# A fused attention and local-attention block: mask, maximum, token shift and value copies each moved to another engine

## What is computed

```python
h = shift_token(x)                      # second half of the channels comes from the token before
q, k, v = split(h @ wqkv)               # 8 heads x 64
q, k = l2norm(q) * qs, l2norm(k) * ksc  # then a rotary turn
sim  = einsum('bhwid,bhwjd->bhwij', bq * 8, bk)   # window of 64 queries x 128 keys
mask = (i < j) | (i > j + WINDOW) | (j == -1)
attn = softmax(where(mask, -max, sim))
x = x + (attn @ bv) @ wo
h = layernorm(shift_token(x))           # the second token shift
x = x + (a * gelu(g)) @ w2 + b2         # a, g = split(h @ w1 + b1)
```

## Time and profile before

| | before |
|---|---|
| median of 3 runs | 2481.74 us (2478.46 to 2484.01) |
| the profiled execution's own time | 2479.8 us |
| its span | 2478.0 us, mean granted clock 0.979 |
| PE busy | 2243.9 us, 91% |
| PEld busy | 1567.1 us, 63% |
| DVE busy | 1675.2 us, 68% |
| ACT busy | 1702.9 us, 69% |
| POOL busy | 1771.1 us, 71% |
| local-attention tiles | 128, the first masked at 222.7 us, the last at 2438.0 us |

### The profile page before, as it was taken

One profiled execution on the slowest core, in us unless ns is written; L12 is line 12 of the kernel. 1 busy time (PEld: TensorE's weight loads), 2 busy tenths in 40 slices (PEclk: granted clock), 3 DMA queues, 4 the chain that ended last, 5 costly groups with the idle time before them and its releaser, 6 DMA issues.

```text
span 2478.0 us, 59154 instructions
## 1 busy us (share of the span) xinstructions
PE 2243.9 (91%) x22208; PEld 1567.1 (63%) x22208; DVE 1675.2 (68%) x3612; ACT 1702.9 (69%) x2766; POOL 1771.1 (71%) x1615
## 2 busy tenths in 40 slices
PE   4888999999999999999999999999999999988887
PEld 1454666676666666666676666666666666665665
DVE  3666766777676776777667676677667766556653
ACT  1455677677777777767777776776777777776663
POOL 2117777786877868777777867777777877788883
PEclk9899999999999999999999999999999999999998
DMA  4221001110110110111011001011111100000000
GB/s 136 62 66 53 29 26 29 44 34 20 42 32 27 36 38 27 26 47 33 22 34 42 27 29 38 22 41 36 33 27 31 45 23 19 8 12 12 2 3 12
DMA packets 74966, 81.99 MB, mean 33 GB/s; under 512 B 7545, under 2 KB 64294, under 8 KB 74674
## 3 DMA queue, kind: packets, MB, share of 16 engines
q1 hardware_dynamic: 74674, 78.04, 11.0%
HBM read 56.26 MB, written 20.97 MB: 31 GB/s over the span
## 4 chain that ended last, share of the span: by engine, by line
PE 50%; ACT 18%; DVE 12%; issue 10%; POOL 8%; DMA 1%; SPq 0%; DVEq 0%; ACTq 0%; POOLq 0%
PE ps L540 8%; PE ps L633 6%; PE ps L825 4%; PE ps L588 4%; PE ps L573 3%; PE ps L700 3%; ACT PT L1188 3%; PE ps L739 3%; PE ps L553 3%; PE ps L722 2%; PE ps L816 2%; DVE ss L1027 2%; DVE nmax L976 2%; POOL inv L1407 2%; PE ps L687 2%
## 5 line engine op out<-in xcount | busy, mean ns | idle before, releaser
L976 DVE TENSOR_REDUCE nmax<-ps 128x1 f32<-128x512 f32 (+3 forms) x1024 | 471.6, 485 | 383.2 <-PE ps L575 380.4
L1188 ACT ACTIVATE PT<-ps 128x512 f32<-128x512 f32 (+1 forms) x768 | 407.0, 533 | 327.7 <-PE ps L590 323.3
L1407 POOL TENSOR_TENSOR inv<-ss,nhalf 128x16 f32<-128x16 f32 x128 | 378.7, 2959 | 322.3 <-DVE QN L1010 322.3
L573 PE MATMUL ps<-KA,QA 72*128 72x512 bf16 (+3 forms) x1024 | 290.2, 310 | 38.4 <-DVE nmax L976 33.1
L1396 POOL TENSOR_TENSOR RS<-RAW,rot 128x512 f32<-128x512 f32 x256 | 324.9, 1290 | 0.0
L1402 POOL TENSOR_TENSOR RC<-RC,RS 128x1024 f32<-128x1024 f32 x128 | 304.0, 2375 | 18.9 <-POOL RS L1396 1.3
L1385 POOL TENSOR_TENSOR RC<-RAW,rot 128x1024 f32<-128x1024 f32 x128 | 307.9, 2405 | 0.0
L588 PE MATMUL ps<-QA,KA 75*128 75x512 bf16 (+3 forms) x1024 | 285.6, 305 | 19.5 <-ACT PT L1188 15.4
L687 PE MATMUL ps<-wqkv,ZT 128*128 128x512 f32 x512 | 242.8, 597 | 0.0
L1246 ACT COPY V_odd<-ps 128x512 f32<-128x512 f32 x128 | 74.9, 585 | 217.1 <-PE ps L700 216.5
L1017 DVE TENSOR_REDUCE nm<-ps 128x8 f32<-128x1024 f32 x128 | 156.2, 1220 | 96.1 <-PE ps L722 95.1
(11 more groups left out here) (130 smaller groups left out, 5674.6 us busy)
## 6 DMA issues: line engine op xcount, KB each, us to landing
QA<-parts SPq DMA_DIRECT2D x192, 96.0 KB
KA<-parts SPq DMA_DIRECT2D x192, 96.0 KB
parts<-qkp SPq DMA_DIRECT2D x32, 384.0 KB, 5.5
X_next<-in_x SPq DMA_DIRECT2D x17, 256.0 KB, 2.9
X<-in_x SPq DMA_DIRECT2D x16, 256.0 KB, 3.0
x_kept<-X SPq DMA_DIRECT2D x16, 256.0 KB, 3.0
XR<-x_kept SPq DMA_DIRECT2D x32, 128.0 KB, 3.7
out<-XR SPq DMA_DIRECT2D x32, 128.0 KB, 1.9
```

The lines of the kernel that those rows point to most:

```text
L573: pe.matmul(dst[:, c0:c0 + w], QA[e][0:QK_ROWS, h % UNIT, qt * P:(qt + 1) * P], KA[e][0:QK_ROWS, h % UNIT, 0:w], start=True, stop=False)
L976: ins = v.tensor_reduce(nmax[:, NT - 1 - r, h % H1:h % H1 + 1], for_max(i, x)[:, c0:c0 + w], AX.X, ALU.max, negate=True)
L1188: a.activation(PT1[:, h % UNIT, c0:c0 + w], for_exp(i, x)[:, 0:w], ACT.Exp, scale=SCALE1).then_inc(exped.sem, 1)
L1407: g.tensor_tensor(inv[:, :], ss[:, :], nhalf[:, :], ALU.pow).then_inc(inv_ready.sem, 1)
```

## The change

- `scores`: the two mask matmuls go. One matmul of a single column stands in their place, and each score matmul starts and stops its own accumulation.
- `maxima`: DVE adds `band` to the scores on their way from PSUM into `PX`, and then reduces `PX` in SBUF to `nm`.
- `exps`: eight exponentials, one for each head of 128 columns, each with its column of `nm` as bias.
- `shift_tokens` leaves PE for SP: two transfers within SBUF, of 127 rows and of 1 row. The DVE copy goes. `norms` and the statistics of the shifted half are split into calls of their own, and `tile_moments` comes after `gate_up` and `heads_over_sum`.
- `v_over`: one copy, to `V_odd`. SP moves its halves to the `V_even` buffers (`move_values`).
- `scores_max` and `scores_exp`: where a chunk holds two tiles, their two causal masks become one matmul of 256 columns.
- POOL: `tile_root` comes after `rotate_by_sin` and the sum.

```diff
+                def move_values(m):
+                    sp.wait_ge(*past(v_ready.sem, v_ready.at(i, m + 1)))
+                    for n, rows in enumerate((slice(0, WIN), slice(WIN, P))):
+                        sp.dma_start(V_even[(m + n) % 2][rows, :, :], V_odd[rows, :, :]).then_inc(v_moved.sem, 16)
+
+                def shift_tokens(m):
+                    l, z, tt = place(m)
+                    dst = XN[m // HT % 2][:, m % HT, D // 2:D]
+                    sp.wait_ge(*past(z_acc.sem, z_acc.at(i, m + 1)))
+                    sp.dma_start(dst[1:P, :], Z[z][0:P - 1, tt, D // 2:D]).then_inc(shifted.sem, 16)
+                    first = Z[z][P - 1:P, tt - 1, D // 2:D] if tt else ident[0:1, D // 2:D]
+                    sp.dma_start(dst[0:1, :], first).then_inc(shifted.sem, 16)
...
+                    if tile_in(i, s - 1):
+                        shift_tokens(s - 1)
                     if s % 2 == 0:
                         u = s // 2 + 10
                         if unit_in(i, u):
                             lay_maxima(u)
                         if unit_in(i, u + 2):
                             lay_out(u + 2)
+                    if tile_in(i, s + 1):
+                        move_values(s + 1)
...
-                                  KA[e][0:QK_ROWS, h % UNIT, 0:w], start=True, stop=False)
-                        last = pe.matmul(dst[:, c0 + w - P:c0 + w], identb[:, :], causal[:, :],
-                                         start=False, stop=True)
-                    last.then_inc(scored.sem, 1)
+                                  KA[e][0:QK_ROWS, h % UNIT, 0:w], start=r == CHUNKS[c][0], stop=False)
+                    n = len(CHUNKS[c])
+                    diagonal = dst[:, c0 + w - n * P:c0 + w].rearrange("p (t x) -> p t x", x=P)
+                    pe.matmul(diagonal, identb[:, :], causal[:, :].unsqueeze(1).to_broadcast([P, n, P]),
+                              start=False, stop=True).then_inc(scored.sem, 1)
...
-                    rows = band[:, 0 if tt else 1, :].unsqueeze(1).to_broadcast([P, PAIR2, P])
-                    for s in range(2):
-                        pe.matmul(ps[:, 2 + s, :], identb[:, :], rows, start=True, stop=False)
+                    pe.matmul(ps[:, 2, 0:1], identb[:, :], band[:, 0, 0:1], start=True, stop=True)
...
-                                               QT[half, j, b * WIN:(b + 1) * WIN], keys, start=False,
-                                               stop=j == PAIR2 - 1)
+                                               QT[half, j, b * WIN:(b + 1) * WIN], keys, start=True, stop=True)
...
-                def shift_tokens(m):
-                    l, z, tt = place(m)
-                    pe.wait_ge(*past(z_acc.sem, z_acc.at(i, m + 1)))
-                    dst = m_ps[:, D:D + D // 2]
-                    mm = pe.matmul(dst, shift[:, :], Z[z][:, tt, D // 2:D], start=True, stop=(tt == 0))
-                    if tt:
-                        mm = pe.matmul(dst, corner[:, :], Z[z][:, tt - 1, D // 2:D], start=False, stop=True)
-                    mm.then_inc(sh_mm.sem, 1)
...
                 def maxima(m):
-                    blocks = sc_ps.rearrange("p (h c) -> p h c", h=H2)
+                    l, z, tt = place(m)
+                    in_heads = "p (h c) -> p h c"
                     v.wait_ge(*past(s_mm.sem, s_mm.at(i, m + 1)))
-                    v.tensor_reduce(nm[:, :], blocks, AX.X, ALU.max, negate=True).then_inc(max_ready.sem, 1)
-                    v.wait_ge(*past(max_ready.sem, max_ready.at(i, m + 1)))
                     v.wait_ge(*past(p_tr.sem, p_tr.at(i, m)))
-                    v.tensor_tensor(PX.rearrange("p (h c) -> p h c", h=H2), blocks,
-                                    nm[:, :].unsqueeze(2).to_broadcast([P, H2, P]),
-                                    ALU.add).then_inc(sub_ready.sem, 1)
+                    v.tensor_tensor(PX.rearrange(in_heads, h=H2), sc_ps.rearrange(in_heads, h=H2),
+                                    band[:, 0 if tt else 1, :].unsqueeze(1).to_broadcast([P, H2, P]),
+                                    ALU.add).then_inc(banded.sem, 1)
+                    v.wait_ge(*past(banded.sem, banded.at(i, m + 1)))
+                    v.tensor_reduce(nm[:, :], PX.rearrange(in_heads, h=H2), AX.X, ALU.max,
+                                    negate=True).then_inc(max_ready.sem, 1)
...
+                def shifted_tokens(m):
+                    l, z, tt = place(m)
+                    v.wait_ge(*past(shifted.sem, shifted.at(i, 2 * (m + 1))))
+                    v.bn_stats(stats[z][:, tt, 6:12], XN[m // HT % 2][:, m % HT, half:D]).then_inc(tile_stats.sem, 1)
...
                     attention_step(s, 3)
+                    if tile_in(i, s + 3):
+                        norms(s + 3)
                     if tile_in(i, s - 1):
-                        tile_moments(s - 1)
-                    elif tile_in(i, s + 3):
-                        norms(s + 3)
+                        shifted_tokens(s - 1)
                     if b:
                         gate_up(p, 0)
                         gate_up(p, 1)
                     if s % 2 and unit_in(i, (s + 17) // 2):
                         heads_over_sum((s + 17) // 2)
+                    if tile_in(i, s - 1):
+                        tile_moments(s - 1)
...
                 def exps(m):
-                    a.wait_ge(*past(sub_ready.sem, sub_ready.at(i, m + 1)))
-                    a.activation(PX, PX, ACT.Exp).then_inc(exp_ready.sem, 1)
+                    a.wait_ge(*past(max_ready.sem, max_ready.at(i, m + 1)))
+                    for h in range(H2):
+                        block = PX[:, h * P:(h + 1) * P]
+                        ins = a.activation(block, block, ACT.Exp, bias=nm[:, h:h + 1])
+                    ins.then_inc(exp_ready.sem, 1)
...
-                    a.copy(V_odd[:, :, 0:E2], heads)
-                    a.copy(V_even[m % 2][0:WIN, :, 0:E2], heads[0:WIN, :, :])
-                    a.copy(V_even[(m + 1) % 2][WIN:P, :, 0:E2], heads[WIN:P, :, :]).then_inc(v_ready.sem, 1)
+                    a.wait_ge(*past(v_moved.sem, v_moved.at(i, 2 * m)))
+                    a.copy(V_odd[:, :, 0:E2], heads).then_inc(v_ready.sem, 1)
...
+                    if tile_in(i, s + 2):
+                        rotate_by_sin(s + 2)
                     if tile_in(i, s - 1):
                         tile_root(s - 1)
-                    if tile_in(i, s + 2):
-                        rotate_by_sin(s + 2)
```

More of the change, by code:

```diff
@@ L192, in build @@
         band = sb("band", [P, 2, P], BF16)
-        shift = sb("shift", [P, P])
-        corner = sb("corner", [P, P])
         cos1 = sb("cos1", [P, S])
@@ L360, in build @@
         v_ready = count("v_ready", ITEMS)
+        v_moved = Landed(nc, ctx, "v_moved", 2 * ITEMS)
         s_mm = count("s_mm", ITEMS)
         max_ready = count("max_ready", ITEMS)
-        sub_ready = count("sub_ready", ITEMS)
+        banded = count("banded", ITEMS)
         exp_ready = count("exp_ready", ITEMS)
@@ L373, in build @@
         z_acc = count("z_acc", ITEMS)
-        sh_mm = count("sh_mm", ITEMS)
-        sh_ready = count("sh_ready", ITEMS)
+        shifted = Landed(nc, ctx, "shifted", 2 * ITEMS)
         tile_stats = count("tile_stats", ITEMS)
@@ L391, in build @@
         y_out = landed("y_out", LANES)
-        N_FIRST, N_CONST = 4, 12 + L * 7
+        N_FIRST, N_CONST = 4, 10 + L * 7
         N_MADE = LANES + 9
@@ L416, in _ @@
                 (causal_t[:, :], t["causal_t"]), (band[:, :, :], t["band"]),
-                (shift[:, :], t["shift"]), (corner[:, :], t["corner"]),
                 (wqkv[:, :, :], t["wqkv"].rearrange("l d n -> d l n")),
@@ L588, in scores_exp @@
                         pe.matmul(dst[:, c0:c0 + w], KA[e][0:ROWS, h % UNIT, kt * P:(kt + 1) * P],
-                                  QA[e][0:ROWS, h % UNIT, kt * P:S], start=True, stop=False)
-                        last = pe.matmul(dst[:, c0:c0 + P], identb[:, :], causal_t[:, :],
-                                         start=False, stop=True)
-                    last.then_inc(scored_t.sem, 1)
+                                  QA[e][0:ROWS, h % UNIT, kt * P:S], start=kt == CHUNKS[c][0], stop=False)
+                    n = len(CHUNKS[c])
+                    diagonal = dst[:, 0:c0 + P].rearrange("p (t x) -> p t x", x=P)[:, ::NT - 1, :]
+                    pe.matmul(diagonal, identb[:, :], causal_t[:, :].unsqueeze(1).to_broadcast([P, n, P]),
+                              start=False, stop=True).then_inc(scored_t.sem, 1)
                 def turn_maxima(s, u):
@@ L734, in attend @@
                     pe.wait_ge(*past(pt_ready.sem, pt_ready.at(i, m + 1)))
-                    pe.wait_ge(*past(v_ready.sem, v_ready.at(i, m + 1)))
+                    pe.wait_ge(*past(v_moved.sem, v_moved.at(i, 2 * (m + 1))))
                     for h in range(H2):
@@ L759, in tokens_over @@
                     if tile_in(i, s - 1):
-                        pe.wait_ge(*past(sh_ready.sem, sh_ready.at(i, s)))
```

(23 more changed lines are left out.)

## The result

The changed kernel takes 2515.8 us (median of 4 runs, 2513.7 to 2518.6) against 2482.4 us for the kernel before on the same chip: ratio 1.0142, 95% interval 1.0118 to 1.0166. It is slower, and 2515.8 lies inside the range; but the growth is 33 us by the medians and 35 by the ratio, where the forecast of 2500 stood 18 above the median of before, and on the profiled executions it is 38.7 us (span 2516.7 against 2478.0) where the terms gave 20.

The account below looks back on a forecast made before the run. ACT's queue was taken to bind odd slots, mostly PE the even ones; +2.8 us a turn gave +18, the last pair +2, so +20 on 2479.8: forecast 2500, own range 2486 to 2530, full range 2405 to 2570.

Parts of the forecast that it names:

- The step on which the sign hung: Odd slots, `exps` to `last_chunk`: ACT's queue binds, so eight exponentials delay `last_chunk` by 1.4 us; faster below 1.15 of growth.
- 0.97: Growth of each odd slot: 1.4 us later on ACT, less 0.43 saved on PE's mask; eight make +7.8 a turn.
- the 2.6 counted for the copies: Start of `values`, where PE waits for ACT: two copies fewer on ACT a slot save 2.6 us a turn.
- some 100 were named: PE over the whole run: busy time was to fall by some 100 us, idle time to grow by more.
- The shift's transfer: SP's 127-row transfer, ahead of DVE's statistics: lands in 5.2 us on one DMA engine, just hidden within about 5.8.
- the rival of the late transfer: Shift's rows at 58 ns a packet land 3.1 us late, DVE stands: +32 us a turn, 2740; chance 0.09.
- the price of POOL's and DVE's new order in the even slots: Two even slots with 0.7 us of slack: `gate_up` behind L1030 takes the bank's gain, +0.2 us a turn.
- the full part lies above its forecast: First tile at 222 us to about 2136: 6.55 turns at +2.8 us, so +18 us.
- The clock: Rival: PE's new idle time lowers its clock, each 0.01 costing 3 us a turn; 2520 to 2560, chance 0.07.
- the 2.3 of the forecast: Slot 8 gains 2.3 us: 0.9 from POOL, 0.5 as the slot before ends later, 0.85 from PE.
- forecast 2.8: One turn of the loop, 16 slots: the terms of odd slots, even slots, slot 8 and copies sum to +2.8 us.
- The tail: Last pair, 8 pairs of slots: POOL's chain binds even slots (-0.6 each), ACT odd ones (+0.8): +2 us.

Follow-up runs that it names:

- e1: The changed kernel with the eight exponentials by head replaced by one over 1,024 columns, using the first head's negated maximum as bias: 2444.5 us, ratio 0.987.
- e2: The changed kernel with the old order back: moments ahead of `gate_up` on DVE, `tile_root` between the rotations on POOL: 2525.2 us, ratio 1.019.
- e3: The changed kernel with DVE's `next_sin` (rope sum) of slots 4 and 12 moved behind `add_mlp`: 2498.1 us, ratio 1.009.
- e5: The changed kernel with the token shift back on PE and its copy back on DVE: 2526.3 us, ratio 1.018.
- e8: The kernel before with only exponentials by head out of PSUM, maximum as bias, so DVE's second pass goes: 2519.5 us, ratio 1.016.
- e10: The changed kernel with the loop over pairs 1 to 5 written out, so no engine jumps back: 2491.6 us, ratio 1.003.
- e7: The changed kernel with mask on PE, one exponential, later rope sum, and POOL's `first_normalise` moved behind slot 8's maxima parts: 2442.6 us, ratio 0.985.
- e12: The changed kernel with mask on PE, later rope sum, no loop; exponentials by head from PSUM in even tiles, one in odd: 2385.8 us, ratio 0.961.

## Why the prediction was right in direction and too small

**Right.** The step on which the sign hung held: ACT's queue binds odd slots, and the growth was sized at 1.4 us and measured at 1.39; e1 takes it away and gives 67 us back. From the start of `exps` to the next `maxima` seven odd slots grew by 0.79 to 0.95 us (0.88 in the mean) against 0.97. Where odd slots begin, `exps` starts 3.2 us sooner, summed over a turn, against the 2.6 counted for the copies; that it is the copies isn't shown, as no run took them back alone. PE's busy time fell by 85 us, where some 100 were named. The shift's transfer was hidden in the full part. DVE waits for it, 3.65 us each time, only in the last four tiles. It was priced at 5.2 us (its own terms, 1.4 us and 127 packets of 29 ns, give 5.1) and lands sooner; in the drain, where it can be followed alone:

```profile
2491.17 0.63 SPq L490
2491.80 0.04 issue
2491.84 3.18 DMA XN<-Z
```

With 1.4 us of it fixed, as the prediction took it, a packet takes 14 ns, not 29. The trace's DMA records say the same: from 1448.0 to 1449.8 the 127 packets of 256 bytes start every 14 ns, at most two under way at a time. So the rival of the late transfer, which needed 33, was far off. One DMA engine for all 127 rows, the case in which the 5.2 us were priced, fits that and the DMA share while it ran (0.09 of sixteen engines, 1.4 engines, between 1448.0 and 1449.7, at 18 GB/s), though no view shows the engines one by one.

**The term that was mis-sized** is the price of POOL's and DVE's new order in the even slots, put at some 0.2 us a turn, where slots 4 and 5 alone took 2.8 us more than forecast: "With POOL rotating through, it should meet the sine in most slots and lose 0.3 to 1 us. In odd slots DVE has room. In even slots `gate_up` stands behind it". The collision was seen, and priced for one small instruction, L1030, at some tenths of a microsecond a turn. The instruction went from 0.38 to 0.73 us in the mean (from 0.18 to 0.70 in the median), as expected. But the same step moved the whole of DVE's work in slot 4 against POOL's, and there a sum of 512 columns took 2.28 us instead of 0.89, with PE waiting for `add_mlp` behind it. PE's wait grew by 1.6 us, and the clock then fell at the head of slot 5, 1.6 us more. Slots 4 and 5 are 3.0 us longer than before; e2 takes 2.8 of it back with the order, and e3 3.6 with the sum alone. Over the six turns that have it that is 18 us, more than the 12.6 that the full part lies above its forecast. As a whole the order isn't a loss (e2's turn is as long): what it wins in slots 2 and 8 hides what it costs here.

**The clock was kept as a rival of its own, with 0.07, and should have been a term of the sum.** The view of waits and windows of before already had it: PE's 2.15 us of wait in slot 8 stood ahead of 3.5 us at half clock. Slot 8 therefore gained 3.9 us, not the 2.3 of the forecast. In the 112 tiles of the full part PE was busy for 36.8 us at a granted clock of 0.5 before and for 55.8 after, by the clock records of the traces; half of that, 18.4 and 27.9 us, is the most that the low clock can have cost. From there to the end it is 10.8 and 18.4 us. Behind the jump the low stretch doubled, from 3.5 to 7 us, and the pair of slots 15 and 0 grew by 2.9 (2.7 over the four jumps) instead of 1.4. Together with what precedes: forecast 2.8, plus 2.8 in slots 4 and 5, plus 1.5 behind the jump, minus 1.6 in slot 8, gives 5.5 of the measured 5.2. The tail, forecast at 2 us and measured at 5.8, lacked the shift's transfer (e5, without it, is 3.0 us shorter from the first of the last 16 tiles to the end) and the clock; how the rest divides isn't shown.

**What stays open.** Why the stretch behind the jump is 7 us in the changed kernel and 3.5 before isn't shown; e8, with the mask and shift matmuls on PE, has 3.5 at three jumps of four, and e5, with the shift alone, has none at three. Nor does the length of a wait decide by itself whether the clock falls: behind the same wait of 2.08 us it fell in six turns of six in the changed kernel and in two of six in e10, behind 2.15 in six of seven before the change, behind 2.64 in three of seven in e2, behind 2.27 in two of seven in e7. The copies and the merged causal masks were not tried by themselves (for the masks the prediction took it that matmuls follow each other at their column rate; in slots of before, bf16 ones of 128 columns start 0.06 us apart and those of 512 take 0.22 to the next), and neither was why 2.3 us come ahead of the first tile.

## What to carry to other kernels

When an engine is freed of a wait, look at what its instructions will now run beside: list every instruction of the neighbour that the traces show held beside it (here the sum of the rope tables, 0.69 us and held 2.28, `XR`, 0.43 and 1.97, and L1030, 0.18 and 0.96), not only the one that happens to stand next, and price each at the full length of what holds it. Then ask who waits behind it. Count PE's waits of about 2 us twice, once for their length and once for the half clock that can follow (here 1.6 us each time that it did, and it did in some turns and kernels only), and put that into the sum as a term with a chance. And where two engines bind different slots, as ACT the odd and PE the even ones here, don't make one edit for both: e12 uses the exponentials by head only in the even slots, where ACT has room, and wins there with the edit that costs 1.1 us in every odd slot of e8.
